# Running states masked in the scan and read as 32x32 tiles, one product for both half-chunks, and a new order of stages

## The chip, the cores and the metric

One Trainium2 chip, one core of it. The metric is the device time of one launch in microseconds, the median of several runs of the same program. The engines named below are TensorE (PE in the profile; PEld are its weight loads), VectorE (DVE), ScalarE (ACT), GpSimd (POOL) and SyncE (SP), which issues the DMA transfers.

## The reference

32 sequences of 512 tokens, 256 features, fp32. A layer norm feeds an attention without softmax (16 heads of 16 features, chunks of 128 tokens), its result is added to x, a second layer norm and the FFN's own norm feed an FFN of 1024 with quantised weights, and half of that plus its input is added again.

```python
q = _phi(proj(Wq, bq)); k = _phi(proj(Wk, bk)); v = proj(Wv, bv)     # _phi = elu + 1
def step(carry, inp):                                   # over chunks of 128 tokens
    S, z = carry; qi, ki, vi = inp
    scores = jnp.where(mask, einsum('bqd,bkd->bqk', qi, ki), 0)      # mask = tril
    num = einsum('bqk,bkd->bqd', scores, vi) + einsum('bqd,bde->bqe', qi, S)
    kcum = jnp.cumsum(ki, axis=1) + z[:, None, :]
    out = num / jnp.sum(qi * kcum, axis=-1, keepdims=True)
    return (S + einsum('bkd,bke->bde', ki, vi), z + ki.sum(axis=1)), out
x = x + attention(layernorm(x));  h = layernorm(x)
x = x + h + 0.5 * (silu(layernorm2(h) @ w1 + b1) @ w2 + b2)
```

## The kernel before

One sequence is a block. A loop runs over the blocks, and each engine has a list of its stages written out by hand; in the pass for block i it does the attention of block i (`A`), the FFN of block i-1 (`Fn`), and the norm and projections of block i+1 (`N`). The passes for blocks 1 to 29 are one hardware loop; the first and last ones stand outside it. Semaphores carry all order between engines: an event is counted, and `w.need(event, shift, k)` waits for its k-th count in a block. `w.hold()` stops TensorE's list until what it has begun is done.

Big products (projections, output projection, the FFN) take fp32 operands split into a high and a low part and run as single-pass products of full 128x128 tiles. The attention's small ones are fp32, and each shows as two matmul records. Heads are 16 features wide, so a pair of heads is 32 partitions (`PW`), four pairs g fill 128, and t counts two halves of the features. A chunk of the reference is worked as two half-chunks r of 64 tokens:
- `k_transposes` (394), and `keys_out` on ScalarE, put the keys by tokens into `k_tok`. `values_out` (876) writes the values into `v_pad`, each pair of heads as [v, 0, 0, v].
- `scores(t)` (408), in 32x64 tiles, one PSUM bank for each g. `mask(t, h)` (627) on VectorE multiplies two of those banks by the causal mask into `probs`.
- `chunk_states(r)` (427): k'v of the half-chunks r, 64 rows by 32 columns, into the bank `kv`. The two row halves write the same place in turn, so the second waits for the first (`half_pe`).
- `sum_states` (636): VectorE's scan adds the half-chunks up along the row into `kv_sums`. `snapshots(t)` (644) multiplies the seven states by the head mask `head_ones`, which zeroes what lies off the diagonal, into `state`, [128, 2, 7, 128].
- `values(t)` (444) adds probs times v into `num`, in 64x32 tiles, row half r into bank r. `from_states(t)` (455) adds state times phi_q: 128 rows by 32 columns, of which only the 32 rows of the pair are not zero.
- `denominators` (467) sums qk = q * cumsum(k) (597, 1002) over the head's features by a product with `head_one`. VectorE takes `reciprocals` (654), and SP spreads them over the partitions as `rb` by 16 transfers (1028). `attention(t)` (662) multiplies num by rb; 918 and 705 split that for `output_projection`.
- The FFN's `fc1(j)` (353, 354) fills two banks for each of 8 slices; ScalarE's `ffn_scaled` (832) and VectorE's `ffn_sum` (617) scale and add them, `ffn_silu` (840) and `ffn_hi` (847) follow, and GpSimd's `ffn_lo` (982) is the low part. `fc2` (287) takes all. VectorE's `residual` (683) and GpSimd's `residual_bias` (997) make the FFN's residual, `input_bias` (988) the attention's. The second norm's factors come from VectorE (736 to 739), and `ffn_norm` (888) on ScalarE makes hn2 from them, which the next pass transposes first (335).

All eight PSUM banks are handed round by the table `BANKS`; `free_bank` lets a stage wait until the bank's last user has been read out (`FREED_BY`). TensorE's list for a full pass:

```python
ffn_in(0); ffn_in(1); k_transposes(0); k_transposes(1); scores(0)
fc1(0); x_transposes(0); x_transposes(1); fc1(1); fc1(2)
chunk_states(0); scores(1); chunk_states(1)
fc1(3); fc1(4); values(0); fc1(5); values(1); from_states(0); from_states(1)
fc1(6); fc1(7); project_kq(); project_v(0); project_v(1); output_projection()
fc2(0); fc2(1); denominators(); fc2(2); fc2(3)
```

## Time and profile before

| | before |
|---|---|
| median of 3 runs | 1490.65 us (1488.85 to 1491.71) |
| the profiled execution | 1494.15 us, span 1492.1 us |
| TensorE matmuls busy | 1414.1 us, 95%, 27482 records |
| VectorE busy | 1233.3 us, 83% |
| ScalarE busy | 1036.8 us, 69% |
| GpSimd busy | 793.0 us, 53% |
| mean granted TensorE clock | 0.98 |
| chain that ended last | PE 78%, DVE 11%, issue 7%, ACT 2%, POOL 1% |

A line of the page's groups gives the source line, engine and operation, what is written from what, shapes, count, then busy time and mean duration, then the engine's idle time just before and what ended it. Durations of TensorE's matmuls overlap, so distances from start to start are the better measure there. Times of a timeline are us from the start of the span. The block whose pass starts at 706.86 serves as the example throughout.

### The profile page before, as it was taken

The numbers are of one execution on the slowest core, as the hardware profiler recorded it, in microseconds if no ns is written. First come the engines' busy times: TensorE is split into PE (matmuls) and PEld (weight loads), VectorE is DVE, ScalarE is ACT, GpSimd is POOL, SyncE is SP. The second block draws the span as 40 slices with busy tenths as digits, with TensorE's granted clock in tenths as the row PEclk, the third lists the DMA queues.
The fourth block names the chain that finished last, engine by engine and source line by source line (L and its number), as shares of the span: only waits on it lengthen the run. The fifth ranks groups of instructions, "written<-read, shape, count | busy, mean of one in ns | idle before, by whom it ended". The sixth has DMA issues, their size and how long they took to land.

```text
span 1492.1 us, 64840 instructions
## 1 busy us (share of the span) xinstructions
PE 1414.1 (95%) x27482; PEld 1231.5 (83%) x27482; DVE 1233.3 (83%) x2077; ACT 1036.8 (69%) x1789; POOL 793.0 (53%) x469
## 2 busy tenths in 40 slices
PE   7669999999999999999999999999999999999978
PEld 7558888888888888888888888888888888888857
DVE  5678888888889888888988888988888898888774
ACT  4357777766777876777776677787677778667643
POOL 2124566545566645456654556664545665455443
PEclk8779999999999999999999999999999999999989
DMA  5111011111101111101111110111110111111010
GB/s 155 38 44 57 25 38 50 56 56 56 52 16 47 54 56 56 56 28 35 50 56 56 56 50 18 47 54 56 56 56 28 35 49 56 56 56 39 11 41 29
DMA packets 83299, 72.13 MB, mean 48 GB/s; under 512 B 14912, under 2 KB 82752, under 8 KB 83264
## 3 DMA queue, kind: packets, MB, share of 16 engines
q1 hardware_dynamic: 81904, 71.62, 15.6%
q8 instruction: 27, 0.44, 0.1%
q10 hardware_dynamic: 1360, 0.01, 0.1%
q14 instruction: 8, 0.07, 0.0%
HBM read 38.03 MB, written 16.78 MB: 37 GB/s over the span
## 4 chain that ended last, share of the span: by engine, by line
PE 78%; DVE 11%; issue 7%; ACT 2%; POOL 1%; DMA 0%; DVEq 0%; ACTq 0%; POOLq 0%
PE sc L287 24%; PE ring L287 18%; PE num L287 6%; DVE state L644 5%; PE sc L408 5%; DVE probs L627 4%; PE sc L353 4%; PE sc L354 3%; PE num L455 2%; PE ring L353 2%; PE ring L394 2%; PE num L335 2%; PE ring L427 2%; ACT silu_f L832 2%; PE ring L354 1%
## 5 line engine op out<-in xcount | busy, mean ns | idle before, releaser
L982 POOL TENSOR_TENSOR s_lo<-silu_f,s_hi 128x512 fp32r<-128x512 f32 x256 | 416.1, 1631 | 565.4 <-ACT s_hi L847 562.2
L840 ACT ACTIVATE silu_f<-silu_f 128x512 f32<-128x512 f32 x256 | 156.4, 622 | 77.1 <-DVE silu_f L617 76.2
L627 DVE TENSOR_TENSOR probs<-sc,causal 128x1024 f32<-128x1024 f32 x128 | 150.8, 1220 | 31.3 <-PE sc L408 31.2
L888 ACT ACTIVATE hn<-x,hn_add,ln_rstd 128x256 f32<-128x256 f32 x128 | 66.5, 591 | 152.9 <-DVE hn_add L736 152.9
L832 ACT ACTIVATE silu_f<-sc,bias,scale 128x512 f32<-128x512 f32 x155 | 120.1, 776 | 63.8 <-PE sc L354 63.6
L847 ACT ACTIVATE s_hi<-silu_f 128x512 fp32r<-128x512 f32 x256 | 158.7, 621 | 1.1
L644 DVE TENSOR_TENSOR state<-kv_sums,head_ones 128x896 f32<-128x896 f32 x64 | 144.5, 2303 | 0.0
L287 PE MATMUL sc<-w_hi,s_hi 128*128 128x256 f32 x496 | 142.8, 288 | 0.0
L353 PE MATMUL sc<-gt_hi,w_q 128*128 128x512 f32 x286 | 122.8, 429 | 21.1 <-DVE probs L627 21.1
L287 PE MATMUL ring<-w_hi,s_lo 128*128 128x256 f32 x496 | 139.9, 282 | 0.0
L287 PE MATMUL ring<-w_hi,s_hi 128*128 128x256 f32 x496 | 139.9, 282 | 0.0
L287 PE MATMUL ring<-w_lo,s_hi 128*128 128x256 f32 x496 | 139.7, 282 | 0.0
L287 PE MATMUL sc<-w_hi,s_lo 128*128 128x256 f32 x496 | 139.6, 281 | 0.0
L287 PE MATMUL sc<-w_lo,s_hi 128*128 128x256 f32 x496 | 139.5, 281 | 0.0
L444 PEld LDWEIGHTS num<-probs,v_pad 64*32 64x32 f32 x8192 | 86.9, 107 | 32.5 <-issue 32.5
L354 PE MATMUL sc<-gt_lo,w_q 128*128 128x512 f32 x286 | 113.7, 398 | 0.0
L597 DVE TENSOR_TENSOR_SCAN qk<-ones,phi_k 128x512 f32<-128x512 f32 x64 | 111.8, 1747 | 2.1
L1002 POOL TENSOR_TENSOR qk<-qk,phi_q 128x512 f32<-128x512 f32 x64 | 109.0, 1722 | 5.6 <-DVE phi_q L588 5.6
L617 DVE SCALAR_TENSOR_TENSOR silu_f<-sc,scale,silu_f 128x512 f32<-128x512 f32 x129 | 93.5, 743 | 21.2 <-ACT silu_f L832 20.8
L444 PE MATMUL num<-probs,v_pad 64*32 64x64 f32 x8192 | 98.4, 230 | 8.1 <-issue 8.1
L997 POOL TENSOR_TENSOR res<-res,bias 128x1024 f32<-128x1024 f32 x32 | 105.1, 3284 | 0.2 <-DVE res L683 0.2
L287 PEld LDWEIGHTS sc<-w_hi,s_hi 128*128 128x128 f32 x496 | 93.3, 188 | 12.4 <-issue 12.4
(186 smaller groups left out, 4270.0 us busy)
## 6 DMA issues: line engine op xcount, KB each, us to landing
x_in<-in_x SPq DMA_DIRECT2D x32, 512.0 KB, 4.0
rb<-den_rows SPq DMA_DIRECT2D x512, 32.0 KB, 1.9
xb<-in_x SPq DMA_DIRECT2D x32, 512.0 KB, 4.7
out<-out_t SPq DMA_DIRECT2D x64, 256.0 KB, 2.4
probs<-in_q SPq DMA_DIRECT2D x2, 512.0 KB, 8.4
silu_f<-in_q SPq DMA_DIRECT2D x2, 512.0 KB, 6.4
res<-in_sc SPq DMA_DIRECT2D x1, 512.0 KB, 6.8
out_t<-in_sc SPq DMA_DIRECT2D x1, 512.0 KB, 9.3
```

Source lines behind the costliest of these rows:

```text
L287: last = e.matmul(target, a, b, start=(n == 0), stop=(n == 3 * len(pairs) - 1))
L353: e.matmul(bank_, w1_q[:, t, cols], gt_hi[:, t, :], start=True, stop=False)
L354: f_pe.done(e.matmul(bank_, w1_q[:, t, cols], gt_lo[:, t, :], start=False, stop=True))
L444: last = e.matmul(num[PW * g:PW * (g + 1), r, num_of(r, t, m)], v_pad[toks, m, t * PAIRS + g, 2 * odd:2 * odd + 2, :], probs[toks, t, g, m ...
L597: kcum.done(e.tensor_tensor_scan(qk[:, t, :], ones[:, 0:1].to_broadcast([P, S]), phi_k[:, t, :], 0.0, ALU.mult, ALU.add))
L627: masked.done(e.tensor_tensor(probs[:, t, 2 * h:2 * h + 2, :, :, :].rearrange("p g m a q -> p (g m a) q"), sc[:, 2 * h:2 * h + 2, :].rearr ...
L644: snap.done(e.tensor_tensor(state[:, t, :, :].rearrange("p n (g x) -> p n g x", x=PW), kv_view[:, t, 0:STATES, :][:, :, None, :].to_broadc ...
L832: f_a.done(e.activation(silu_f[:, j % SLOTS, :], use_bank(f"f{j}a"), ACT.Identity, bias=bias_1[:, j:j + 1], scale=scale_1[:, 0, j:j + 1]))
L840: silu.done(e.activation(slot, slot, ACT.Silu))
L847: sh.done(e.activation(s_hi[:, j, :], silu_f[:, j % SLOTS, :], ACT.Copy))
L982: sl.done(e.tensor_tensor(s_lo[:, j, :], silu_f[:, j % SLOTS, :], s_hi[:, j, :].bitcast(F32), ALU.subtract))
L1002: qkcum.done(e.tensor_tensor(qk[:, t, :], qk[:, t, :], phi_q[:, t, :], ALU.mult))
```

## The change

The head mask is put into the scan: `sum_states` now computes (previous + new) x `state_keep`, where `state_keep` holds the parity of the partition's head in place of `head_ones` and a zero at the end of each row of eight. The result, [128, 512], is `state`, and `snapshots` goes. `from_states` takes the 32 rows by 32 columns of a pair, with a stride of 8 elements in the weights, and a `hold` stands ahead of it. `v_pad` has twice the size: for each r the rows of the other half stay zero, so one product over all 128 rows gives both half-chunks side by side, and `chunk_states` is one stage. `denominators` sums 128 columns for each chunk m with both t in one accumulation; `den_rows` is [128, 128], the reciprocal half as wide, and `rb` is filled by 8 transfers that repeat each row 16 times. `BANKS` is new, `free_bank` sorts its waits, mask(1, 1) runs ahead of mask(1, 0), and all engines' lists have a new order. ScalarE loads the table of Silu after exponential(3), not at the start of a pass.

```diff
-        v_pad = sb("v_pad", [P, C, T * PAIRS, 4, HD])
+        v_pad = sb("v_pad", [P, 2, C, T * PAIRS, 4, HD])
         probs = sb("probs", [P, T, PAIRS, C, 2, HALF])
-        kv_sums = sb("kv_sums", [P, S])
-        state = sb("state", [P, T, STATES, P])
+        state = sb("state", [P, S])
...
+            "ht0": (6,), "ht1": (1,), "kt0": (0,), "kt1": (7,), "sc0": (2, 3, 4, 5), "f0a": (1,), "f0b": (0,), "xt0": (6,),
+            "xt1": (3,), "f1a": (2,), "f1b": (1,), "kv": (7,), "f2a": (0,), "f2b": (6,), "sc1": (2, 3, 4, 5),
+            "num": (0, 1), "f3a": (7,), "f3b": (4,), "f4a": (6,), "f4b": (5,), "f5a": (2,), "f5b": (4,), "f6a": (5,),
+            "f6b": (2,), "f7a": (7,), "f7b": (6,), "k0": (3,), "q0": (4,), "k1": (7,), "q1": (0,), "v0": (1,), "v1": (2,),
+            "wo0": (6,), "wo1": (5,), "z0": (4,), "den": (0,), "z1": (2,),
...
+        MASKED = ((0, 1), (3, 2))
...
-                if r == 0:
-                    free_bank(w, "kv", present)
-                else:
-
-                    w.need(half_pe, 0)
-                w.hold()
-                toks = slice(HALF * r, HALF * (r + 1))
+                free_bank(w, "kv", present)
                 for t in range(T):
                     for m in range(C):
                         for g in range(PAIRS):
-                            last = e.matmul(kv_bank[PW * g:PW * (g + 1), t, :, 2 * m + r],
-                                            k_tok[toks, m, t * P + PW * g:t * P + PW * (g + 1)],
-                                            v_pad[toks, m, t * PAIRS + g, 0:4:3, :],
+                            last = e.matmul(kv_bank[PW * g:PW * (g + 1), t, :, 2 * m:2 * m + 2].rearrange("p x r -> p r x"),
+                                            k_tok[:, m, t * P + PW * g:t * P + PW * (g + 1)],
+                                            v_pad[:, :, m, t * PAIRS + g, 0:4:3, :],
                                             start=True, stop=True, skip_group_check=True)
-                (half_pe, upd_pe)[r].done(last)
+                upd_pe.done(last)
...
             def from_states(t):
-                w.need(snap, 0, t)
+
+                w.need(summed, 0)
+                w.hold()
                 for c in range(1, 2 * C):
                     m, r = divmod(c, 2)
                     for g in range(PAIRS):
-                        last = e.matmul(num[PW * g:PW * (g + 1), r, num_of(r, t, m)],
-                                        state[:, t, c - 1, PW * g:PW * (g + 1)], phi_q[:, t, chunk(r, m)],
+                        pair = slice(PW * g, PW * (g + 1))
+                        last = e.matmul(num[pair, r, num_of(r, t, m)],
+                                        state_view[pair, t, c - 1, :], phi_q[pair, t, chunk(r, m)],
                                         start=False, stop=False, skip_group_check=True)
                 if t == T - 1:
                     num_pe.done(last)
...
-                    for half in range(2):
-                        g = 2 * t + half
-                        last = e.matmul(use_bank("den")[32 * g:32 * g + 32, 0:2 * P], head_one[:, :],
-                                        qk[:, t, 2 * P * half:2 * P * (half + 1)], start=True, stop=True,
+                    for m in range(C):
+                        last = e.matmul(use_bank("den")[32 * m:32 * m + 32, 0:P], head_one[:, t, :, :, :],
+                                        qk[:, t, m * P:(m + 1) * P], start=(t == 0), stop=(t == T - 1),
...
             fc1(1)
+            chunk_states()
             fc1(2)
-            chunk_states(0)
             scores(1)
-            chunk_states(1)
+            values(0)
             fc1(3)
             fc1(4)
-            values(0)
+            values(1)
             fc1(5)
-            values(1)
             from_states(0)
             from_states(1)
...
-                kv_sb.done(e.tensor_tensor_scan(kv_sums[:, :], scan_keep[:, :], use_bank("kv"), 0.0, ALU.mult, ALU.add))
...
+                summed.done(e.tensor_tensor_scan(state[:, :], use_bank("kv"), state_keep[:, :], 0.0, ALU.add, ALU.mult))
...
+            input_lo(1)
             ffn_sum(1)
-            input_lo(1)
+            sum_states()
+            mask(1, 1)
             ffn_sum(2)
             mask(1, 0)
-            mask(1, 1)
-            sum_states()
             ffn_sum(3)
-            snapshots(0)
-            snapshots(1)
             ffn_sum(4)
             ffn_sum(5)
+            residual()
+            ffn_sum(6)
             attention(0)
             attention(1)
-            ffn_sum(6)
             ffn_sum(7)
             if preparation[3]:
                 preparation[3]()
             attention_lo(0)
+            attention_lo(1)
             if N2:
                 ve_norm_x(e, w, 2)
-            residual()
-            attention_lo(1)
             features(0)
             cumulate(0)
             features(1)
+            features(2)
             add_residual(0)
-            features(2)
             cumulate(1)
             features(3)
...
-                for h in range(2):
+                for r in range(2):
+                    toks = slice(HALF * r, HALF * (r + 1))
                     last = e.activation(
-                        v_pad[:, 2 * n + h, :, 0:4:3, :],
-                        use_bank(f"v{n}")[:, h * D:(h + 1) * D].rearrange("p (r a x) -> p r a x", a=2, x=HD),
-                        ACT.Copy)
+                        v_pad[toks, r, 2 * n:2 * n + 2, :, 0:4:3, :].rearrange("p c g a x -> p (c g) a x"),
+                        use_bank(f"v{n}")[toks, :].rearrange("p (c a x) -> p c a x", a=2, x=HD), ACT.Copy)
...
             ffn_silu(1)
-            ffn_silu(2)
             ffn_hi(1)
             ffn_scaled(3)
+            ffn_silu(2)
+            ffn_hi(2)
             ffn_scaled(4)
-            ffn_hi(2)
             ffn_silu(3)
+            ffn_hi(3)
             ffn_scaled(5)
-            ffn_hi(3)
             ffn_silu(4)
+            ffn_hi(4)
             ffn_silu(5)
             ffn_scaled(6)
-            ffn_hi(4)
+            ffn_hi(5)
             ffn_scaled(7)
+            ffn_silu(6)
+            ffn_hi(6)
             attention_hi(0)
-            ffn_silu(6)
-            ffn_hi(5)
+            attention_hi(1)
             ffn_silu(7)
-            ffn_hi(6)
-            if N:
-                e.activation(table_warm[:, 0:1], ones[:, 0:1], ACT.Exp)
-            attention_hi(1)
+            table_exp()
             exponential(0)
             ffn_hi(7)
             exponential(1)
             exponential(2)
+            values_out(0)
             exponential(3)
-            values_out(0)
+            table_silu()
+            values_out(1)
             q_by_parity(0)
-            values_out(1)
...
+            ffn_lo(0)
+            input_bias()
+            ffn_lo(1)
+            ffn_lo(2)
+            ffn_lo(3)
+            ffn_lo(4)
+            ffn_lo(5)
+            residual_bias()
+            ffn_lo(6)
+            if N2:
+                po_norm(e, w, 2)
+            ffn_lo(7)
+            query_sums(0)
+            query_sums(1)
+            ln2_factors()
...
-                    for half in range(2):
-                        g = 2 * t + half
-                        for a in range(DUP):
-                            e.dma_start(rb[a:P:DUP, t, 2 * P * half:2 * P * (half + 1)], den_rows[32 * g:32 * g + 32, :])\
-                                .then_inc(rb_in.sem, 16)
+                    for m in range(C):
+                        rows = den_rows[32 * m + t * HT:32 * m + (t + 1) * HT, :]
+                        e.dma_start(rb[:, t, m * P:(m + 1) * P], rows[:, None, :].to_broadcast([HT, HD, P]))\
+                            .then_inc(rb_in.sem, 16)
...
+            own = state_keep[:, :].rearrange("p (t a y) -> p t a y", t=T, a=2)
+            e.tensor_tensor(own, own, parity[:, None, :, None].to_broadcast([P, T, 2, S // (2 * T)]), ALU.mult)\
+                .then_inc(p_par, 1)
+            e.wait_ge(p_par, 3)
+            e.memset(state_keep[:, 2 * C - 1:S:2 * C], 0.0).then_inc(p_par, 1)
```

## Rows read from the trace of the kernel before

**Rows 1.** The page's first part: busy time, share of the span and count of instructions.

```profile
PE 1414.1 (95%) x27482; PEld 1231.5 (83%) x27482; DVE 1233.3 (83%) x2077; ACT 1036.8 (69%) x1789; POOL 793.0 (53%) x469
```

**Rows 2.** Timeline of TensorE where two blocks begin: start, duration, engine, line, operation.

```profile
177.99 0.49 PE L335 MATMUL num<-ident,hn 128*128 128x128 f32 x3
...
1367.93 1.04 PE L335 MATMUL num<-ident,hn 128*128 128x128 f32 x8
```

**Rows 3.** Stretches of from_states (line 455): length, busy PE and PEld, granted clock, DMA.

```profile
723.43:724.24 0.81, 0.81 (x56) 0.81 (x56) 1.00 0.00 0
...
724.57:725.35 0.78, 0.78 (x56) 0.78 (x56) 1.00 0.00 0
```

**Rows 4.** Timeline of TensorE in the example block, from fc1(1) on.

```profile
711.66 0.48 PE L353 MATMUL sc<-gt_hi,w_q 128*128 128x512 f32 x1
...
713.82 0.75 PE L427 MATMUL ring<-v_pad,k_tok 64*32 64x32 f32 x64
...
714.60 1.20 PE L408 MATMUL sc<-q_mask,phi_k 32*64 32x128 f32 x64
...
715.73 0.76 PE L427 MATMUL ring<-v_pad,k_tok 64*32 64x32 f32 x64
...
716.42 0.50 PE L353 MATMUL num<-gt_hi,w_q 128*128 128x512 f32 x1
...
716.99 0.40 PE L353 MATMUL ring<-gt_hi,w_q 128*128 128x512 f32 x1
...
717.22 0.40 PE L354 MATMUL ring<-gt_lo,w_q 128*128 128x512 f32 x1
...
718.34 0.50 PE L353 MATMUL sc<-gt_hi,w_q 128*128 128x512 f32 x1 [0.72 <-DVE probs L627]
...
719.47 1.49 PE L444 MATMUL num<-probs,v_pad 64*32 64x64 f32 x128
...
720.89 0.51 PE L353 MATMUL sc<-gt_hi,w_q 128*128 128x512 f32 x1
...
723.43 2.13 PE L455 MATMUL num<-phi_q,state 128*32 128x64 f32 x112
...
725.49 0.50 PE L353 MATMUL ring<-gt_hi,w_q 128*128 128x512 f32 x1
```

**Rows 5.** Timeline of VectorE in the same block: masks, one ffn_sum, snapshots.

```profile
710.06 2.36 DVE L627 TENSOR_TENSOR probs<-sc,causal 128x1024 f32<-128x1024 f32 x2 [0.43 <-PE sc L408]
...
712.33 0.74 DVE L617 SCALAR_TENSOR_TENSOR silu_f<-num,scale,silu_f 128x512 f32<-128x512 f32 x1
...
715.93 2.35 DVE L627 TENSOR_TENSOR probs<-sc,causal 128x1024 f32<-128x1024 f32 x2 [0.34 <-PE sc L408]
...
719.97 4.55 DVE L644 TENSOR_TENSOR state<-kv_sums,head_ones 128x896 f32<-128x896 f32 x2
```

**Rows 6.** Timelines of GpSimd and VectorE where both work: this block and the last one.

```profile
720.48 5.13 POOL L982 TENSOR_TENSOR s_lo<-silu_f,s_hi 128x512 fp32r<-128x512 f32 x2 [2.19 <-ACT s_hi L847]
...
1443.26 4.30 DVE L683 TENSOR_SCALAR res<-x,res_mul,res_add 128x256 f32<-128x256 f32 x4
...
1443.59 3.82 POOL L982 TENSOR_TENSOR s_lo<-silu_f,s_hi 128x512 fp32r<-128x512 f32 x3 [0.95 <-ACT s_hi L847]
```

**Rows 7.** Groups of instructions by form: count, busy us, mean ns, idle time before.

```profile
L654 DVE RECIPROCAL den_rows<-sc 128x256 f32<-128x256 f32 x32 | 56.2, 1757 | 41.3 <-PE sc L467 41.3
...
L876 ACT ACTIVATE v_pad<-sc 128x256 f32<-128x256 f32 x128 | 41.4, 378 | 5.6 <-PE sc L287 5.6
...
L636 DVE TENSOR_TENSOR_SCAN kv_sums<-scan_keep,ring 128x512 f32<-128x512 f32 x32 | 38.7, 1211 | 2.1 <-PE ring L427 2.1
```

**Rows 8.** Waits between 134 and 1367.9: who waited for whom, us, times, longest.

```profile
ACT hn L888 <- DVE hn_add L736: 126.4, 28, 4.6
```

**Rows 9.** Timeline of TensorE in the last block with attention: the output projection begins.

```profile
1448.21 0.58 PE L287 MATMUL sc<-wo_hi,gt_hi 128*128 128x256 f32 x1 [6.86 <-DVE gt_lo L705]
```

**Rows 10.** The stretch of values (line 444) in block 0, as in rows 3.

```profile
43.37:51.95 8.58, 4.05 (x256) 3.59 (x256) 0.50 0.38 126
```

More of the change, by code:

```diff
@@ L75, in build @@
     SLOTS = 4
-    DUP = 32 // HT
     WARM, WARM_BETWEEN = 22, 5
@@ L356, in fc2 @@
             def fc2(c, shift=-1):
+                if not Fn or (A and not N and c == C - 1):
+                    return
                 n, h = divmod(c, 2)
@@ L493, in pe_iteration @@
                 ready_qk()
-                project_kq()
+                for n in range(2 * T):
+                    project_kq(n)
                 bias_products()
@@ L1132, in _ @@
             count(e.memset(ones[:, :], 1.0))
-            for tile_, value in ((head_ones, 1.0), (causal, 1.0), (causal_2, 1.0), (head_one, 1.0)):
-                count(e.memset(tile_[:], value))
+            for tile_, value in ((head_ones, 1.0), (causal, 1.0), (causal_2, 1.0)):
+                count(e.memset(tile_[:, :], value))
+            count(e.memset(head_one[:, :, :, :, :], 0.0))
+            e.wait_ge(p_const, made)
+            for t in range(T):
+                count(e.memset(head_one[:, t, :, t, :], 1.0))
             count(e.memset(minus_half[:, :, :], -0.5))
@@ L1156, in _ @@
             po_norm(e, Waiter(e, -1), 1)
-            count(e.memset(v_pad[:, :, :, :, :], 0.0))
+            count(e.memset(v_pad[:, :, :, :, :, :], 0.0))
             po_norm(e, Waiter(e, -1), 2)
@@ L1239, in bias_products @@
                         n = D + t * FT + j
-                        last = e.matmul(bank(1)[:, n:n + 1], w1_q[:, t, j * P:(j + 1) * P].bitcast(F32),
+                        last = e.matmul(bank(SPARE)[:, n:n + 1], w1_q[:, t, j * P:(j + 1) * P].bitcast(F32),
                                         beta_c[:, t:t + 1], start=True, stop=True)
```

169 lines of the change are left out of this document (85 added, 84 removed), and 6 rows, old and new, of the table BANKS.

## The prediction, made before the changed kernel ran

> **What bounds the kernel now.** I read the page's busy shares first: TensorE is busy for 95% of the span [rows 1]. The next question is whether the missing part and the slack inside "busy" can move, so I went to TensorE's timeline. The first matmul of the FFN's transposes (line 335) marks the start of a block. From the block at 177.99 to the one at 1367.93 there are 27 blocks [rows 2]: 1189.94 / 27 = 44.07 us each, at full granted clock (1.00) [rows 3]. So 30 of the 32 blocks are one pattern and TensorE's list sets its length, and a change is worth what it takes out of that list, times about 30, plus something at both ends.
>
> Inside one block I took the distance from the start of one stage to the start of the next, because durations of pipelined matmuls overlap [rows 4]:
> - fc1(1) and fc1(2): 711.66 to 713.82 = 2.16. First half of chunk_states to 714.60 = 0.78. scores(1) to 715.73 = 1.13. Second half to 716.42 = 0.69. Together 4.76.
> - fc1(3) and fc1(4): 716.42 to 719.47 = 3.05, with a hole in it. Two matmuls follow each other in 0.23 (716.99 to 717.22), so the next was due at 717.45 and starts at 718.34, released by a mask on VectorE: 0.89 of waiting. The four matmuls of fc1(4) then take 1.13 (718.34 to 719.47), which holds a slow first step after the break; one such block for both, 1.13 + 4 x 0.23 = 2.05, would be the stage without the hole. So 1.00 is lost.
> - from_states: 723.43 to 725.49 = 2.06. Seen in two stretches [rows 3], its 56 records for t=0 end at 724.24, the 56 for t=1 start at 724.57. The gap of 0.33 ends when VectorE's snapshot products end (719.97 + 4.55 = 724.52) [rows 5]. Within a stretch one record takes 0.80 / 56 = 14.2 ns. (Each fp32 matmul is two records.)
>
> **The change part by part.**
> 1. The snapshot products go (line 644, 4.55 us of VectorE a block) [rows 5]. Nothing replaces them: the mask rides in the scan that was there anyway. VectorE is not the bound, so only the 0.33 gap in from_states counts: -0.33. GpSimd, which ran two of its products in 5.13 beside them where three in a row elsewhere take 3.82, gets faster too [rows 6], off the path.
> 2. chunk_states becomes one stage of 32 products (64 records) with 128 rows, 32 columns and 64 moving columns. from_states before has exactly this shape, so 64 x 14.2 ns = 0.91, and 0.12 for the change to the next stage, what is left of from_states (2.06 less 0.33 less 112 x 14.2 ns = 0.14) rounded down. About 1.03 in place of 0.78 + 0.69. The product itself gains nothing: half as many records, each twice as long. What is gained is one change of stage. The new stretch fc1(1), chunk_states, fc1(2), scores(1) is 1.13 + 1.03 + 1.13 + 1.13 = 4.42 against 4.76: -0.34.
> 3. New order: values(0) moves ahead of fc1(3), sum_states and mask(1,1) ahead of ffn_sum(2), and mask(1,0) behind it. Is the hole of 1.00 closed? From the start of scores(1) TensorE reaches values(1) after 1.13 + 1.42 (values(0), 719.47 to 720.89) + 2.05 = 4.60. VectorE's chain from the same point: the first mask starts 1.33 after scores(1) (714.60 to 715.93), two masks take 2.35, one ffn_sum lies between them (0.74 at most), so the last mask is done after 1.33 + 2.35 + 0.74 = 4.42, and the release takes 0.06 (715.93 + 2.35 = 718.28 to 718.34) [rows 4, 5]. 4.48 against 4.60: in time, by 0.12. The banks of fc1(3) and fc1(4) come free earlier than that in the same chain. The scan before it is not late: it stands behind the masks of scores(0) (over at 710.06 + 2.36 = 712.42, so 5.6 into a block that starts at 706.86) and four operations of at most 0.74, so it starts by 8.5, when chunk_states (about 6.0 to 7.0) is over. It lasts 1.21 [rows 7], to 9.7 at the latest; scores(1) starts near 8.1, so its mask could start at 9.5. By durations alone that is 0.2 late, but each operation begins about 0.09 before its predecessor's end (masks over at 712.42, the next began at 712.33 [rows 5]), five times here, which makes it early. So -1.00.
> 4. x_transposes(1) now takes bank 3 and waits for mask(0,0), which ends near 710.06 + 1.18 = 711.24, plus a release. The four transposes it holds come right ahead of fc1(1) at 711.66 [rows 4, 5], so they were due at about the same time: +0.04.
> 5. from_states in 32x32 tiles, from states kept with a stride of 8 elements. Columns and count stay: four tiles at a time, 64 columns each. No row shows this tile or such a stride. Downward it is bounded by itself: no tile of the trace does 64 columns faster than 4 x 14.2 = 57 ns a record, so no gain. Upward, if tiles of different row groups did not overlap, each record would take that 57 ns alone. I take 14.2, because the nearest rows (the same four column groups, the same data moved) are that; the far end is rival B. Its added hold costs what the hold before values costs, 0.10, and is inside the distances used.
> 6. Denominators: 16 records with 128 columns in place of 8 with 256, on the same four column groups: 0. VectorE's reciprocal halves (1.76) [rows 7]: about -0.8, off the path, and the factors of the second norm come earlier. SP issues 8 transfers of rb in place of 16, with the same bytes; they are needed 20 us later: 0.
> 7. ScalarE: v_pad is written by two operations of 512 elements on 64 partitions in place of two of 256 on 128 (0.38 each) [rows 7]. Cost grows with elements and at most doubles: up to +0.38 each, 1.5 a block, plus the table load that moves in front of values_out(1). ScalarE waits 126.4 / 28 = 4.5 a block for the norm's factors [rows 8], which covers both. Uncovered, they would delay hn2 and cost up to 1.5 a block.
> 8. GpSimd: input_bias now stands ahead of ffn_lo(1), and behind it wait sl(1) to sl(3) and with them ffn_scaled(5) to (7). Following the list by the steps above, each comes in time: 0, at most rival A.
>
> Sum for a block: -0.33 - 0.34 - 1.00 + 0.04 = -1.63, so about 42.4 in place of 44.07. Times 30 = -48.9.
>
> **Ends.** Block 0 has no FFN work; its two values stages take 8.58 for 256 records at half the granted clock [rows 10], 34 ns each where a block in the middle needs 1.42 / 128 = 11, with the engine waiting for nothing the profile names. I read that as instructions that come late. 64 records of the block go; at 34 ns that is -2. The last block with attention waits 6.86 for attention_lo(1), which stands behind a residual that took 4.30 for four operations of VectorE [rows 6, 9]. In the new order the residual is earlier and attention follows at once: about half of the wait goes, -3.5. A longer zeroing of v_pad and two steps for the new masks: under +0.5, beside waits. Together -54.4. The profiled execution lasted 1494.15: it becomes 1439.8. Against the median of the runs shown (1490.65, 3.5 lower) the same subtraction gives 1436.3. I take the middle, **1438**.
>
> **Rivals.**
> A. *The gap moves* (1448 to 1470). Two places are tight. The mask before values(1) has 0.12 of room. And residual now runs while GpSimd works through its s_lo products. What happens then stands in the last block: four operations took 4.30 beside three s_lo products of 3.82 together [rows 6]. Here that would be 3 us on VectorE in front of ffn_sum(6) and attention. q1 needs attention's bank 4.2 us after the projections start, which I find reached with about 0.2 to spare, and the denominators' input would come within 0.3 of its time. Against it: that room exists, and off-path delays cost nothing. If a half microsecond a block leaks back: 30 x 0.5 = 15, so 1453. The same class holds a from_states slowed by its stride (20 ns in place of 14.2: +0.65 a block, 1458).
> The Trainium skill has a rule for this collision: by the GPSIMD Engine Reference, section 1 (Specifications), GpSimd shares its SBUF interfaces with VectorE and contends with its two-port modes and with instructions of two SBUF inputs. The trace agrees: 5.13 for two products beside the snapshot product, whose inputs are both in SBUF.
> B. *Slower: 32x32 tiles do not overlap* (1590). The two stages whose tiles lie in different row groups, scores and values, send each row group to a bank of its own, and the old chunk_states put its second row half behind a wait. In the new from_states four row groups write one bank at once, at different partitions; no row shows that to be concurrent. At one record at a time, 112 x (57 - 14.2) ns = +4.8 a block, times 32 = +153, on top of 1438 gives about 1590. It decides from 28.8 ns a record (14.2 + 1.63 / 112), that is two at a time: there the whole change is worth nothing, about 1490.
> The page TensorEngine Tiling of the Trainium skill, section Restrictions and Gotchas, says that different row tiles cannot access the same PSUM bank simultaneously. Taken literally that is this rival. Its page on the PSUM (PSUM bank collisions raise a hardware error) narrows the clash to one bank in one quadrant of 32 partitions, which the diagonal tiles avoid. No run here shows either.
> C. *The change does not do what it says*: the scan's mask costs TensorE a later start of from_states, or the hole is not the mask's, and 1.00 a block stays: 1468. The release of 718.34 is named by the profile, so this is small.
>
> **How the numbers follow.** Forecast case 1428 to 1448: 0.60. Below 1428 (one more leftover closes at an end): 0.05. A: 0.20. C: 0.04. B and everything down to no gain: 0.11, of which 0.01 lies within 0.2% of 1490.65, about what a measurement of this kernel tells from no change. So faster 0.90, same 0.01, slower 0.09 (0.01 of B's case is a small gain). The range for 8 in 10 reaches from a microsecond or so below the forecast case to the far side of A: **1426 to 1466**.
>
> **What the new profile should show.** Blocks of 42.4 us between first matmuls of the hn2 transposes. No wait of TensorE for a mask beyond 0.1. from_states as one run of 112 records in about 1.6, chunk_states 64 in about 0.9. VectorE's busy share falls from 83% by about 10 points (4.5 + 0.8 of 44 us). Wrong signs: from_states records above 20 ns (B or its mild form), VectorE's residual at 3 us or more a block and a wait of q1 for attention (A), a wait left of about 1 us in fc1 (C). The prediction fails if the spacing of small matmuls in the new tile shape is not that of the old one.

## The result and the profile after

The changed kernel took **1619.6 us** (median of 4 runs, 1611.6 to 1625.4) against 1491.2 for the kernel before (1488.9 to 1493.5) on the same chip: a ratio of **1.086, 95% interval 1.080 to 1.092**. Predicted were 1438 us and "faster" with a chance of 0.90. Both the sign and the size are wrong.

The page's first part of the changed kernel answers to [rows 1]:

```profile
PE 1451.2 (90%) x25690; PEld 1264.6 (78%) x25690; DVE 1151.3 (71%) x2014; ACT 1084.1 (67%) x1789; POOL 687.4 (43%) x473
```

TensorE has 1792 fewer matmul records, is busy for 37 us longer, and its share falls from 95% to 90%. From the chain of work that ended last, first line, before and then after:

```profile
PE 78%; DVE 11%; issue 7%; ACT 2%; POOL 1%; DMA 0%; DVEq 0%; ACTq 0%; POOLq 0%
```

```profile
PE 87%; issue 10%; DVE 2%; ACT 1%; POOL 1%; DMA 0%; DVEq 0%; ACTq 0%; POOLq 0%
```

The other engines nearly leave the chain; TensorE and "issue", time in which nothing the profile shows was waited for, take their place. A block, measured as in [rows 2], lasts 48.4 us instead of 44.07 (188.4 to 1496.3, 27 blocks, 46.8 to 53.7 each). TensorE's waits over the loop of the changed kernel (who <- whom, us in total, times, longest):

```profile
PE ring L340 <- issue: 55.6, 28, 3.3
PE sc L416 <- issue: 18.2, 21, 1.8
PE num L460 <- issue: 16.6, 28, 1.1
PE num L446 <- issue: 13.3, 23, 1.1
PE ring L429 <- issue: 1.8, 3, 0.9
```

That is 105.5 us, 3.8 a block, and no wait for a mask, a state or a DMA is in the list. TensorE's timeline in the block at 766.59:

```profile
766.59 0.67 PE L340 MATMUL ring<-ident,hn 128*128 128x128 f32 x4 [1.67 <-issue]
...
768.50 0.45 PE L416 MATMUL sc<-q_mask,phi_k 32*64 32x128 f32 x8
769.87 1.14 PE L416 MATMUL sc<-q_mask,phi_k 32*64 32x128 f32 x56 [0.92 <-issue]
...
773.96 1.10 PE L429 MATMUL ring<-v_pad,k_tok 128*32 128x64 f32 x64
...
777.27 0.71 PE L446 MATMUL num<-probs,v_pad 64*32 64x64 f32 x47
778.77 1.04 PE L446 MATMUL num<-probs,v_pad 64*32 64x64 f32 x81 [0.79 <-issue]
```

The stages run at the usual pace between the stops: chunk_states is 64 records in 1.03 us from start to start, and the second scores go at 14.9 ns a record. But a stage of many small products stops in its middle, and the first product of the block comes 1.67 late, with nothing outstanding. The line that explains it is in the page's part on DMA queues (packets, MB, share of 16 engines), before and then after:

```profile
q8 instruction: 27, 0.44, 0.1%
```

```profile
q8 instruction: 278, 4.55, 1.1%
```

Packets of 16 KB. In the kernel before, 13 come up to the end of the loop's first pass, 14 after the loop, none between 118 and 1367 us. In the changed kernel 9 come in each of the 28 repeated passes (28 x 9 + 26 = 278). The block above starts again at 815.2; over 766 to 815 the view of DMA traffic has:

```profile
q8 instruction: 9, 0.15, 1.2%
```

### The profile page after: what moved, and what is told of

Same layout as the page of the kernel before. It is cut to its first block, busy times and chain, and to the rows that moved or that the text cites. A ratio compares the mean times of both kernels' runs of the same rounds, so it can differ in the third digit from the quotient of the medians.

```text
span 1612.6 us, 60915 instructions
## 1 busy us (share of the span) xinstructions
PE 1451.2 (90%) x25690; PEld 1264.6 (78%) x25690; DVE 1151.3 (71%) x2014; ACT 1084.1 (67%) x1789; POOL 687.4 (43%) x473
## 4 chain that ended last, share of the span: by engine, by line
PE 87%; issue 10%; DVE 2%; ACT 1%; POOL 1%; DMA 0%; DVEq 0%; ACTq 0%; POOLq 0%
PE sc L292 34%; PE num L446 6%; PE ring L292 5%; PE num L292 5%; PE sc L416 5%; PE num L460 4%; PE sc L358 4%; PE sc L359 3%; PE num L358 3%; PE ring L358 3%; PE ring L359 2%; PE ring L429 2%; PE num L359 2%; PE ring L340 1%; PE num L474 1%
## 5 line engine op out<-in xcount | busy, mean ns | idle before, releaser
L292 PE MATMUL sc<-w_hi,s_hi 128*128 128x256 f32 x992 | 285.9, 288 | 1.5
L292 PE MATMUL sc<-w_lo,s_hi 128*128 128x256 f32 x992 | 280.5, 283 | 0.0
L292 PE MATMUL sc<-w_hi,s_lo 128*128 128x256 f32 x992 | 280.2, 282 | 0.0
L292 PEld LDWEIGHTS sc<-w_hi,s_hi 128*128 128x128 f32 x992 | 189.7, 191 | 12.5 <-issue 12.5
L292 PEld LDWEIGHTS sc<-w_lo,s_hi 128*128 128x128 f32 x992 | 190.0, 191 | 0.0
L292 PEld LDWEIGHTS sc<-w_hi,s_lo 128*128 128x128 f32 x992 | 190.0, 191 | 0.0
L705 DVE TENSOR_TENSOR gt_lo<-rb,gt_hi 128x512 fp32r<-128x512 f32 x64 | 112.4, 1795 | 6.4 <-ACT gt_hi L916 6.4
L830 ACT ACTIVATE silu_f<-ring,bias,scale 128x512 f32<-128x512 f32 x93 | 71.6, 769 | 59.5 <-PE ring L359 59.4
L416 PE MATMUL sc<-q_mask,phi_k 32*64 32x128 f32 x4096 | 90.2, 291 | 18.9 <-issue 18.9
L416 PEld LDWEIGHTS sc<-q_mask,phi_k 32*64 32x64 f32 x4096 | 68.8, 137 | 42.6 <-issue 42.6
```

Source lines behind the costliest of these rows:

```text
L292: last = e.matmul(target, a, b, start=(n == 0), stop=(n == 3 * len(pairs) - 1))
L416: last = e.matmul(sc[HALF * r:HALF * (r + 1), g, m * P:(m + 1) * P].rearrange("p (a q) -> p a q", a=2), phi_k[rows, t, chunk(r, m)], q_mas ...
L705: at_l.done(e.tensor_tensor(gt_lo[:, t, :], rb[:, t, :], gt_hi[:, t, :].bitcast(F32), ALU.subtract))
L830: f_a.done(e.activation(silu_f[:, j % SLOTS, :], use_bank(f"f{j}a"), ACT.Identity, bias=bias_1[:, j:j + 1], scale=scale_1[:, 0, j:j + 1]))
```

## Experiments on the instructions

**Theory T.** I counted TensorE's instructions in the built programs (an fp32 product is 4, two weight loads and two matmuls; other products and transposes 2; the rest 1). The count gives 1748 and 1636 for a pass of the loop, and the traces have that many records between two loop branches. The whole list is 7115 long before and 6669 after: 27.8 and 26.05 pieces of 256, for 27 and (without the refetches) 26 packets. So a packet is 256 instructions of TensorE's, called a piece below. T says: the loop stays in the engine only if it touches no more than 7 pieces (it is then called resident). The changed loop is shorter, but the list ahead of it has shrunk as well, and it begins at another place in its piece. Rivals: R1, the 32x32 tiles are slow; R2, the new order puts dense stages together and outruns the supply; R4, program size; R5, any padding helps.

**after_pad128** puts products that do nothing ahead of the loop:

```diff
                 keep_busy(WARM_BETWEEN)
+                for _ in range(32):
+                    e.matmul(bank(SPARE)[0:32, 0:32], ident[0:32, 0:32], ident[0:32, 0:32], start=True, stop=True,
+                             tile_position=(0, 0))
```

> The changed kernel with 32 tiny products (32x32, 4 TensorE records each, so 128 instructions) put ahead of the loop, in the wait before the first projections; nothing else differs. Theory T (instructions): a pass of the loop has 1636 TensorE instructions, 6.4 pieces of 256 (one piece is the 16 KB packet of the instruction queue, at 64 bytes each); by where the loop begins it touches 7 pieces or 8, and with 8 it is fetched again in each pass. Counted from the build, and with the piece ends placed where the two traces show packets asked for, the changed kernel's loop touches 8, the padded one 7. T expects about 27 instruction packets in all instead of 278, first scores at 15 ns per record instead of 30 to 36, a block of 42.4 us instead of 48.3, and 1430 to 1450 us. Rival R1 (the 32x32 tiles are slow), R2 (the new order puts the dense stages back to back and outruns the instruction supply) and R4 (the program's size) each expect 1615 to 1625 us and some 278 packets: neither tiles, order nor size got smaller.

Measured: 1483.1 us, ratio 0.9927 (0.9903 to 0.9952). Its page and its timeline at the same stages:

```profile
q8 instruction: 26, 0.43, 0.1%
```

```profile
712.64 1.10 PE L429 MATMUL ring<-v_pad,k_tok 128*32 128x64 f32 x64
713.67 0.50 PE L358 MATMUL num<-gt_hi,w_q 128*128 128x512 f32 x1
...
714.81 1.21 PE L416 MATMUL sc<-q_mask,phi_k 32*64 32x128 f32 x64
```

136 us gone by adding 128 instructions, with tiles, order and all other work unchanged. R1, R2 and R4 fall. But 1483 is not the 1430 to 1450 that was expected: the blocks are 43.61, not the 42.4 that T alone would leave; the section after this one is on that.

**after_pad256** (`range(64)` in the same place) and **before_pad64** (`range(16)`, in the kernel before):

> The same with 64 tiny products, 256 instructions: exactly one piece more ahead of the loop, so that the loop lies as it does in the changed kernel. T expects 1615 to 1635 us and 9 instruction packets per pass again. If padding helped by itself (a warmer start, another phase between the engines, rival R5), this kernel would be as fast as the one with half of it, 1430 to 1450.

> The kernel before with 16 tiny products, 64 instructions, ahead of the loop. Its loop has 1748 TensorE instructions, 6.8 pieces, and begins a few instructions behind a piece's start; 64 later it touches 8 pieces. T expects instruction packets in every pass (9 or 10, some 280 in all) and a kernel slower by 5 to 9%, 1565 to 1625 us. R1, R2 and R4 expect no change: 1489 to 1494 us and 27 packets.

Measured, one run each: 1630.6 us with 279 packets, and 1724.1 with 280. R5 falls: twice the padding brings the slow time back. And the kernel before, whose work is untouched, becomes 15% slower (expected 5 to 9%), its blocks 52.0 us. Its waits over the loop are of the same kind:

```profile
PE num L455 <- issue: 54.7, 28, 2.3
PE num L335 <- issue: 50.5, 28, 2.1
PE sc L408 <- issue: 31.8, 16, 3.2
PE num L444 <- issue: 27.0, 36, 1.2
```

**warm10** takes 12 warm-up products away instead of adding any:

```diff
-    WARM, WARM_BETWEEN = 22, 5
+    WARM, WARM_BETWEEN = 10, 5
```

> The changed kernel without any padding, but with 10 warm-up products at its start in place of 22: 48 TensorE instructions fewer ahead of the loop. From the packets of the runs so far the piece ends lie where an instruction's number, divided by 256, leaves 199 to 236. The changed kernel's loop ends at instruction 3308, 8 to 37... behind such an end (3271 to 3308); 48 earlier it ends at 3260, ahead of it, and touches 7 pieces. T expects the padded kernel's time without padding: 26 or 27 packets, 1479 to 1486 us. If it was not the place but the extra products themselves that helped, it stays at 1610 to 1625.

Measured in one run: 1475.5 us, 26 packets (a little better than expected; the padding is not there to run). All kernels with one rule, pieces beginning at instruction 256n + x, where these results leave 190 to 230 for x:

| kernel | loop, first to last instruction | pieces touched | packets | us |
|---|---|---|---|---|
| before | 1766 to 3514 | 7 | 27 | 1491 |
| changed | 1672 to 3308 | 8 | 278 | 1620 |
| after_pad128 | 1800 to 3436 | 7 | 26 | 1483 |
| after_pad256 | 1928 to 3564 | 8 | 279 | 1631 |
| before_pad64 | 1830 to 3578 | 8 | 280 | 1724 |
| warm10 | 1624 to 3260 | 7 | 26 | 1475 |

For 1748 instructions only 45 of 256 places are good, for 1636 there are 157. The kernel before sat in the narrow good window, the changed one fell just outside a wide one. The x of the rule is fitted to these results; the places of the packets had given 199 to 236 before warm10 ran, and warm10 came out as that said.

The stops cost clock as well. TensorE's granted clock over the loop is 1.00 in the kernel before and in after_pad128, but 0.98 in the changed kernel, 0.99 in after_pad256 and 0.96 in before_pad64. In the changed kernel ten stretches of the loop, 44 us together, have 0.50 (1.2 GHz); the 16 of its 27 blocks that have none of them still last 47.8 us on average. So of the 4.8 us that a block loses (48.4 against 43.61), 4.2 are lost at full clock and about 0.7 come with the lower one. In before_pad64 31 such stretches add up to 123 us; at most half of that, 61 us, of its 229 us over the kernel before can be the clock.

The Trainium skill has part of what the prediction lacked. By its page Runtime: NRT & Kernel Launch, section Instruction fetch mechanics, TensorE's instruction memory holds 2048 instructions, is refilled in blocks of 256, and the next block is fetched while the current one runs. Seven blocks of a loop and one fetched ahead would fill those eight, which agrees with every line of the table. The same section calls the cost mostly hidden; here the measurement decides: 4.8 us of 48.4 a block (against 43.61 resident) and 7.9 of 52.0 (against 44.07), the lower clock included.

## Experiments on the remaining 45 us

**The hole ahead of fc2(0).** With instructions resident TensorE has one hole per block. Its timeline and its waits in after_pad128:

```profile
736.88 0.28 PE L292 MATMUL sc<-wo_hi,gt_lo 128*128 128x256 f32 x1
737.94 0.36 PE L292 MATMUL sc<-w_hi,s_hi 128*128 128x256 f32 x1 [0.78 <-POOL s_lo L989]
```

```profile
PE sc L292 <- POOL s_lo L989: 17.5, 26, 0.9
```

And VectorE and GpSimd ahead of it:

```profile
723.74 4.01 DVE L686 TENSOR_SCALAR res<-x,res_mul,res_add 128x256 f32<-128x256 f32 x4
...
734.53 0.17 DVE L573 TENSOR_SCALAR ve<-mv 128x4 f32<-128x4 f32 x1
...
736.64 0.73 DVE L600 SCALAR_TENSOR_TENSOR phi_q<-sc,bias_qk,clip 128x512 f32<-128x512 f32 x1
```

```profile
720.78 6.50 POOL L989 TENSOR_TENSOR s_lo<-silu_f,s_hi 128x512 fp32r<-128x512 f32 x5
...
734.86 1.02 POOL L979 TENSOR_TENSOR rstd<-ve,minus_half 128x4 f32<-128x4 f32 x1 [3.36 <-DVE ve L573]
735.85 1.94 POOL L989 TENSOR_TENSOR s_lo<-silu_f,s_hi 128x512 fp32r<-128x512 f32 x1
```

Two things end almost together: s_lo(7), behind a norm factor that waits 3.36 us for VectorE, and phi_q, which frees bank 4 for z0. Both could come from the residual, 4.01 us for four operations beside GpSimd. **lo7_first** takes the first away on GpSimd, **residual_late** the suspected cause:

```diff
             ffn_lo(6)
+            ffn_lo(7)
             if N2:
                 po_norm(e, w, 2)
-            ffn_lo(7)
```

```diff
             ffn_sum(5)
-            residual()
             ffn_sum(6)
...
             attention_lo(0)
-            attention_lo(1)
             if N2:
                 ve_norm_x(e, w, 2)
+            residual()
+            attention_lo(1)
...
-            residual_bias()
             ffn_lo(6)
...
             ffn_lo(7)
+            residual_bias()
```

> The padded changed kernel with one line of GpSimd's list moved: the s_lo product of fc1 group 7 stands ahead of the norm factor of the next input (rstd), not behind it. In the padded kernel TensorE has one hole per block, 26 times, 24.7 us together (0.95 each), in front of fc2(0), which needs all s_lo. Theory U: it is a chain of lists. VectorE's residual, 4.9 us for four operations beside GpSimd's s_lo products, makes the statistics of the next input late; GpSimd waits for them in rstd, and s_lo(7) stands behind that. U expects the hole to close to 0.2 or less, blocks of 42.7 to 43.0 us in place of 43.6, and 1455 to 1465 us in place of 1483. Rival V: the hole is bank 4, which z0 takes over from q0 and which is free only when VectorE has read it (phi_q, over 0.5 us before the hole ends): then it shrinks by some 0.5 at most, 43.3 and about 1470. Rival W: ScalarE's s_hi(7) is as late as the norm, and nothing changes, 1480 to 1486.

> The padded changed kernel with the residual put back where the kernel before has it: VectorE's four operations behind the statistics of the next input and ahead of attention_lo(1), and GpSimd's bias on it behind the last s_lo. U expects the residual at 0.4 us per operation again (1.6 to 2.0 for four), rstd some 2 us earlier, the hole ahead of fc2(0) gone and blocks of 42.7 to 43.0 us, 1455 to 1465 in all, if the later attention_lo(1) does not open a hole before the output projection. If the collision with GpSimd plays no part (the statistics are late for another reason), the hole stays at 0.95 and the time at 1480 to 1486.

lo7_first: 1475.4 us in one run, blocks 43.55 (V expected 43.3, U 42.7 to 43.0), the hole still there 25 times with 13.6 us in the view of waits (17.5 before), now named

```profile
PE sc L292 <- DVE phi_q L600: 13.6, 25, 0.7
```

So the list on GpSimd was not the cause of more than a small part (43.61 to 43.55 a block): rival V, the bank, holds the hole when s_lo(7) is out of the way. residual_late, one run: **1452.7 us** (1455 to 1465 expected), blocks 42.70, no hole ahead of fc2(0). Its VectorE timeline:

```profile
717.25 0.17 DVE L573 TENSOR_SCALAR ve<-mv 128x4 f32<-128x4 f32 x1
717.34 1.39 DVE L686 TENSOR_SCALAR res<-x,res_mul,res_add 128x256 f32<-128x256 f32 x4
```

The residual takes 1.39 there and 4.01 in its new place. The view of its line in after_pad128 (ns min/median/max) shows where that comes from:

```profile
L686 DVE TENSOR_SCALAR res<-x,res_mul,res_add x4: 403/1181/1478, 723.7 to 727.4; 128x256 f32<-128x256 f32 x4
```

The three long ones start while GpSimd's five s_lo run (720.78 to 727.28), the one of 403 ns starts at 727.4, when GpSimd is idle until 727.84. Over the whole trace, 105 operations of the residual in after_pad128 run beside an s_lo, with a median of 1.38 us; the 24 others have 0.40. What both ends of the hole share is a VectorE that arrives late, and moving this one step takes 0.91 a block away. How much of it is the collision and how much the place in the list, the run alone does not separate, but the traces say something for bank 4. In both kernels the same operations of VectorE stand ahead of q0's phi_q. Over 25 blocks they last 28.6 us a block in after_pad128 and 26.1 in residual_late, and 2.4 of these 2.5 are the residual's; phi_q ends 30.7 and 30.0 us after the start of its block. So what makes this end late is that the residual is slower, not that it stands earlier. For the norm factor and s_lo(7) both count: the residual stands ahead of them in one list and behind them in the other.

**The first pass.** In after_pad128 the first denominators start at 40.74 (before: 29.13) and the first product of block 0 at 44.5 (33.3). TensorE's denominators and ScalarE's list there:

```profile
40.74 1.08 PE L474 MATMUL num<-qk,head_one 128*32 128x128 f32 x16 [8.71 <-POOL qk L1008]
```

```profile
30.63 1.20 ACT L878 ACTIVATE v_pad<-num 64x512 f32<-64x512 f32 x2 [5.87 <-PE num L292]
31.85 0.69 ACT L856 ACTIVATE clip<-num,bias_qkm 128x512 f32<-128x512 f32 x1
```

The new order has values_out(0) ahead of exponential(3). In the loop I see no cost of it. In the first pass TensorE reaches v's projections at 28.92, behind the k and q projections and the products for the biases, and ScalarE waits 5.87 us for them; the exponential, phi_q, the query sums and the denominators stand behind that. **exp3_early**, and **both_fixes** with lo7_first's edit as well:

```diff
+            if not A:
+                exponential(3)
             values_out(0)
-            exponential(3)
+            if A:
+                exponential(3)
```

> The padded changed kernel with ScalarE's list changed in its first pass alone: exponential(3) ahead of values_out(0) there, as in the kernel before; the loop stays. In the padded kernel the first denominators start at 40.7 us against 29.1 before, and block 1 starts at 89.9 against 81.0. Theory X: exponential(3) stands behind values_out(0), which in the first pass waits for the late projections of v, and phi_q, the query sums and the denominators wait for it. X expects the denominators 7 to 10 us earlier, block 1 at 80 to 84, and 1474 to 1477 us in place of 1483. If the start is late for the instructions (the theory T of the first runs) or for the padding itself (5 us at most), little changes: 1481 to 1485.

> Both edits together: s_lo(7) ahead of the norm on GpSimd, and exponential(3) ahead of values_out(0) in the first pass. With U and X the gains add up: 26 x 0.9 + 8 = 31 us less than the padded kernel, 1448 to 1456 us, a ratio near 0.973 to the kernel before. If the two mechanisms hide one another or another wait takes over (attention at q1's bank, ScalarE), 1460 to 1475.

exp3_early: denominators at 33.51, block 0 from 36.89, block 1 from 82.6 instead of 89.9, so X holds for the start. But the time of its one run is 1480.0, not 1474 to 1477: the blocks are 43.92 instead of 43.61, with the same list. both_fixes: 1475.4, ratio 0.9868 (0.9839 to 0.9897), far from the 1448 to 1456 that U and X together gave. The blocks of exp3_early lose 8.4 us over 27, and 6.6 of it are two waits that after_pad128 has too: TensorE waits 21.0 us instead of 17.5 for s_lo, and 4.0 instead of 0.9 for attention (`rb`), which frees a bank. Why a start 7 us earlier makes these waits longer stays open.

**Without the hole** the two add up. **best_pad** is residual_late with exp3_early, **best_warm10** the same with 10 warm-up products and no padding:

> The padded changed kernel with the residual back in its old place on VectorE and GpSimd (1452.7 alone) and exponential(3) ahead of values_out(0) in ScalarE's first pass (block 1 began 7.3 us earlier alone). If these are separate, about 1446 us (1443 to 1449), a ratio near 0.968 to the kernel before, blocks of 42.7. If the gain of the first pass is given back in block 1, as it was when the first pass alone was changed, 1450 to 1454.

> The same two edits with 10 warm-up products and no padding. T expects 26 or 27 instruction packets and blocks of 42.7; its start has no padding to run, so 0 to 4 us less than the padded one, 1440 to 1448. If the place is wrong, 9 packets a pass and 1570 to 1590.

1444.2 us, ratio 0.9672 (0.9653 to 0.9691), and **1443.1 us, ratio 0.9671 (0.9645 to 0.9698)**, both with 26 packets. Each beats both kernels. They are not the changed kernel with only the place of its loop put right: the residual and the first exponential are back where the kernel before has them. The page of best_warm10:

```profile
PE 1392.9 (97%) x25666; PEld 1233.0 (86%) x25666; DVE 1073.0 (74%) x2014; ACT 1083.6 (75%) x1789; POOL 724.8 (50%) x473
```

**What the parts are worth.** **before_states** is the kernel before with the masked scan and from_states in 32x32 tiles alone; **before_product** adds chunk_states in one stage of products with zeroed halves; **values_late** is best_warm10 with `values(0)` behind `fc1(4)` again. All touch 7 pieces; each ran once, so they are compared by their blocks. The blocks of the first two are all alike, within 0.2 us.

```diff
-                        last = e.matmul(num[PW * g:PW * (g + 1), r, num_of(r, t, m)],
-                                        state[:, t, c - 1, PW * g:PW * (g + 1)], phi_q[:, t, chunk(r, m)],
+                        last = e.matmul(num[pair, r, num_of(r, t, m)],
+                                        state_view[pair, t, c - 1, :], phi_q[pair, t, chunk(r, m)],
...
-            snapshots(0)
-            snapshots(1)
```

```diff
-            chunk_states(0)
+            chunk_states()
...
-            chunk_states(1)
```

```diff
             scores(1)
-            values(0)
             fc1(3)
             fc1(4)
+            values(0)
```

> The kernel before with one part of the change alone: the states masked in the scan and used in 32x32 tiles; VectorE's snapshot products go, everything else and every order stays. Its loop has 1750 TensorE instructions in place of 1748 and begins 2 later, still on 7 pieces. The prediction's step was -0.33 us a block; the fed changed kernel shows records of 15.6 ns in place of 14.2, so theory: from_states 1.88 us in place of 2.06, records of 15.6 ns, the 0.89 hole ahead of fc1(4) still there, blocks of 43.9 and 1484 to 1490 us. Rival B of the prediction (tiles that do not overlap) expects 28.8 ns a record or more and 1495 us upward.

> The kernel before with the masked states (blocks of 43.82 us as measured) and, on top, chunk_states as one stage of products with halves of v zeroed, at the place of the first of the two old stages; every other order as before. Its loop has 1620 TensorE instructions and touches 7 pieces. By the prediction's step alone the block loses 0.34 (43.4 to 43.5). Theory: without the new order it gains nothing, because the hole ahead of fc1(4) ends with a mask that is timed from scores(1): the stage that goes away behind scores(1) only makes the hole longer (0.89 to 1.5 or 1.6), and the longer first stage (1.03 in place of 0.78) pushes scores(1) back, so 43.9 to 44.15 us a block, 1489 to 1497 us in all.

> The best version so far (10 warm-up products, the two edits; blocks of 42.70 us) with one part of the new order undone: values(0) stands behind fc1(4) again, as in the kernel before. The count and the place of TensorE's instructions stay. If the order closed the hole as the prediction worked out, it opens again: the masks on VectorE follow scores(1) as before, so fc1(3) and fc1(4) reach banks that are not yet read, and the block grows by 0.8 to 1.1 us, to 43.5 to 43.8, with one wait of TensorE for a mask per block; 1466 to 1474 us in all. Rival: the hole was closed by VectorE's new order alone (the scan ahead, ffn_sum between), and the block stays within 0.2 of 42.70.

before_states: 1487.5 us (the kernel before 1492.3 beside it), blocks 43.82 (-0.25), 112 records from 720.35 to 722.08, 15.6 ns each, the hole ahead of fc1(4) in place:

```profile
720.35 1.95 PE L456 MATMUL num<-phi_q,state 32*32 32x64 f32 x112
722.23 0.50 PE L352 MATMUL ring<-gt_hi,w_q 128*128 128x512 f32 x1
```

before_product: 1488.4 us (the kernel before 1487.9 beside it, one run), blocks 44.07, so 0.25 worse than before_states. The mask is timed from scores(1), which now comes 0.25 later behind the longer chunk_states (1.03 against 0.78), and the wait for it grew from 0.72 to 1.41, by the 0.69 of the stage that was removed behind scores(1):

```profile
713.51 0.40 PE L353 MATMUL ring<-gt_lo,w_q 128*128 128x512 f32 x1
715.31 0.51 PE L352 MATMUL sc<-gt_hi,w_q 128*128 128x512 f32 x1 [1.41 <-DVE probs L621]
```

values_late: 1481.4 us, blocks 43.80, 1.10 more than best_warm10, with the mask's wait back (27 times, 20.1 us). The time is above the expected 1466 to 1474; what the blocks do not explain lies in the passes at both ends (the last two blocks 46.0 and 46.3 us instead of 44.4 and 43.7):

```profile
711.13 0.50 PE L358 MATMUL sc<-gt_hi,w_q 128*128 128x512 f32 x1 [0.74 <-DVE probs L636]
```

## Why the prediction was wrong, point by point

- **What bounds the kernel: the step that failed.** "TensorE's list sets its length" took it for granted that the list is delivered. That held in the kernel before by 45 places in 256. The prediction counted the instructions that go (64 in block 0) but never asked where the loop then lies. The evidence was in its own rows: 34 ns a record in block 0 [rows 10], read there as "instructions that come late" and used only for -2 at the start. Resident and at full clock, the same records start every 10.0 ns. Block 0 has half the clock; twice 10.0 is 20, an estimate, and some 14 of the 34 are left for instructions that come late. The term that was left out is the 136 us between the changed kernel and its padded twin (1619.6 to 1483.1), 2.5 times the whole predicted gain of 54.4 and of the other sign. The sign of failure that the prediction named, another spacing of the new tiles, did not come.
- **Rival A: right in kind, too small and in another place.** The prediction expected the residual to take 3 us more beside GpSimd's s_lo; it took 4.01 instead of 1.39, so 2.6 more. But q1's wait for attention is small (0.9 us in two blocks of after_pad128). What came late was s_lo(7) and z0's bank, held by phi_q, at 0.91 a block instead of the 0.5 of the prediction: 1483.1 against 1452.7 for residual_late. The Trainium skill's rule from the GPSIMD Engine Reference that stands beside rival A has nothing in these runs against it: the same operation takes 0.40 with GpSimd idle and 1.48 at most with it at work. The residual has only one tensor from SBUF, so of the rule's two cases only the two-port mode could be meant, and no run shows the mode.
- **States, 32x32 tiles: right, a little dear.** -0.33 predicted, -0.25 measured (the stage itself 1.88 instead of 2.06; the other 0.07 is not located). The records take 15.6 ns, not 14.2: groups of four start every 62 ns, 6 apart within a group and 43 from one group to the next. **Rival B falls**: at 28.8 it would have cancelled the gain. The 128x32 tiles start in the same way, 6 to 7 apart and then 36. By the 0.23 us that 512 moving columns take in a full tile, 64 would take 29 ns, an estimate; so at 15.6 more than one of the tiles must be at work, each with its own row group and all with one bank, at different partitions. The rule of the Trainium skill's page TensorEngine Tiling, section Restrictions and Gotchas, taken literally, does not fit these records; the narrower one of its PSUM page agrees with them.
- **One product: 1.03 predicted for the stage, 1.03 measured.** But its -0.34 was entered as a term of its own. Without the new order it costs 0.25. That it pays with the new order fits the sum below, but no run has that order without it.
- **The mask hole: right.** -1.00 predicted; it is gone in every padded version, and moving values(0) back alone brings 1.10 back. The margin of 0.12 held: no mask is among the waits of TensorE's matmuls in after_pad128, residual_late or best_warm10.
- **x_transposes(1): +0.04 predicted,** about +0.2 measured (in after_pad128 the second four start 0.62 after the first four, 711.13 to 710.51, where 0.44 is due, and have one more slow step of 0.06).
- **Sum for a block:** -1.63 predicted, -1.37 measured in residual_late and best_warm10 (42.70). The missing 0.26 is the 0.16 of from_states and part of the last point.
- **Ends.** Block 0 became shorter by 2.3 (from its first transposes to block 1: 47.7 before, 45.4 in after_pad128), -2 predicted. The last block with attention lost 4.1 (49.56 to 45.42), of which 0.46 is what every block lost, so 3.7 against 3.5. What was missed is the pass ahead of block 0: +11.3, of which exp3_early takes 7.7 back. Step 7 looked at ScalarE's slack in the loop and not at its list in the first pass, where the same order waits for v's projections, the last that TensorE does there before the denominators.
- **VectorE's share** was to fall by 10 points: 83% before, 78% in after_pad128 with its slow residual, 74% in best_warm10.
- **The time.** 1443 with all three faults out, 1438 predicted. The steps inside the block were nearly right; the answer was not. Two faults, the place of the loop and the first pass, lay outside the steady block that was summed up; the third, the slow residual, was seen as rival A and left out of the sum.

## What to carry to other kernels

Before shrinking or growing a program with a long loop, count the engine's instructions: how many 256-instruction pieces the loop touches is decided by its length and by what stands ahead of it, and a page whose instruction packets grow with the passes says that the loop is not resident. When it is not, add or drop a few idle instructions ahead of the loop before judging the change. And read a new order twice, for the steady state and for the first pass, and price a removed stage only together with the wait that follows it.

## What was not expected of the hardware

- A loop of 1636 TensorE instructions ran at 43.6 or at 48.4 us a pass, one of 1748 at 44.07 or 52.0, by its place alone. Not resident, it took 9 packets a pass, where it touches 8 pieces.
- A loop that is not resident shows as busy time too, not as idle time alone: TensorE's 1406 us in after_pad128 are 1451 in the changed kernel, which has the same work. Part of that is the clock: 0.50 in ten stretches, 44 us, of its loop.
- 32x32 tiles on the diagonal, in groups of four into one bank, ran at 15.6 ns a record where 128x32 tiles took 14.2.
